# Attention kernel: softmax denominators from probabilities added on VectorE and GpSimd instead of TensorE, and x in one buffer

## The chip, the cores and the metric

The program runs on one core of a Trainium2 chip. The metric is the device time of one execution in microseconds (us); lower is better. PE is TensorE, DVE VectorE, ACT ScalarE, POOL GpSimd, and SP the queue that issues most transfers.

## What is computed

The program is a decoder of six stages: linear plus softmax attention, a graph and router stage, a mixture of experts, a second self-attention, a causal cross-attention with keys and values from a context, and a gated network. The change lies in the second self-attention (four batches of 512 positions, 16 heads of 32) and in the cross-attention (the same sizes, causal). What they compute:

```python
# self-attention of x after layernorm (four batches)
scores = jnp.einsum('bhqd,bhkd->bhqk', q, k) * scale
p = jax.nn.softmax(scores, axis=-1)
o = jnp.einsum('bhqk,bhkd->bhqd', p, v)
return jnp.einsum('bsd,ed->bse', o, w_o)
...
# cross-attention, keys and values from the context
scores = jnp.einsum('bhqd,bhkd->bhqk', qh, kh) * inv_sqrt_d
scores = jnp.where(causal, scores, jnp.finfo(scores.dtype).min)
attn = jax.nn.softmax(scores, axis=-1)
out = jnp.einsum('bhqk,bhkd->bhqd', attn, vh)
```

## The kernel before, in words

Both stages are one function, `attention_layers`. It runs 32 **steps** g: batch b = g // 4 (0 to 3 self-attention, which I call plain; 4 to 7 cross-attention, causal) and c = g % 4, a group of four heads. Each step has eight **half-tiles** s: key tile t = s // 2 and pair of heads w = s % 2. All engines run written-out orders over g and s; semaphores tie them together.

In half-tile s of step g, PE issues `scores_kq(g, s)` (keys on partitions, L440), then `scores_qk(g + 1, s)` for the next step (queries on partitions, L420, in causal steps with a mask product, L425), and then `half(g, s - 2)`: for even s it is `weigh`, four products of the probabilities of one key tile with v (L454); for odd s it is `add_up`, four products of the same probabilities with ones (L463), which sum them over the keys. The last two halves of a step fall into half-tiles 0 and 1 of the next. Behind half-tile 7, `turn_maxima` (L431) turns the row maxima of step g + 1, and `project(g + 3)` makes queries and keys of step g + 3 (L50 to L52).

DVE takes the row maxima of every qk pair (`maxima`, L657). When the last is out, PE may turn them: `turn_maxima` waits for `maxima(g + 1, 7)`. Between the maxima DVE has the reciprocals of the sums of step g - 1 (L682, half-tiles 2 to 5), in steps with c = 0 the layernorm statistics of the next batch (L635, half-tiles 2 to 5), and in steps with c = 1 the residual additions, the normalisation (L649) and the low halves of the turned x (L718). ACT takes the exponentials of every kq pair into `probs` (L572), which has two buffers of a key tile. POOL multiplies the weighed values by the reciprocals (`at_oT`, L766), and in causal steps clears what lies above the diagonal (L750).

The scores, projections, values and outputs share three pairs of PSUM banks in turn. A kq pair is free when ACT has taken its exponential, a qk pair when DVE has its maxima, and PE can run no further ahead than that: the qk pair of half-tile s reuses the banks of the kq pair of s - 1, and the kq pair of s those of the qk pair of s - 2. PE has extra work in some half-tiles (`UNITS`): outputs of the previous batch (L532) in steps with c = 1, the turn of x (L496) there too, and v of the next batch in half-tile 3 of the steps with c = 2 and c = 3.

The x of a batch lies in one of two buffers of 1 MB, `shared_x`.

## Time and profile before

| what | value |
|---|---|
| median of 3 runs | 2982.72 us (2970.9 to 2985.78) |
| profiled execution | 2978.98 us, of which the span of the trace is 2977.2 us |
| the two stages in the trace | about 1500 to 2435 us of the span |
| PE busy in them, from 1600 to 2300 us | 93 to 98 us of each 100 |
| DVE busy there | 52 to 62 us of each 100 |

Times in rows are microseconds from the start of the span. In a row of the timeline the first number is the start, the second the duration, then engine, line, operation and tiles; a bracket at its end gives how long the engine sat idle before it and what released it. A record of the form `x8` on L454 or L463 is one group of four products (each is recorded as two passes). Instructions of one engine overlap a little at their ends, so a start-to-start distance is the better price of one in a row of many.

### The profile page before, as it was taken

What the parts mean: (1) busy time and instruction counts of PE and PEld (TensorE: products, weight loads), DVE (VectorE), ACT (ScalarE), POOL (GpSimd) and SP (SyncE); (2) the same over time, 40 slices, a digit from 0 to 9 for tenths busy, and PEclk for the clock granted to TensorE, in tenths of its full rate; (3) what the DMA queues carried; (4) which work ended last, traced back from release to release, by engine and by line L of the source; (5) the groups of instructions that cost most, each with busy time, mean ns of one, the idle gap of its engine ahead of it and who ended that gap; (6) DMA issues with size and microseconds to landing.
All of it is one profiled execution on the core that took longest, in us unless ns stands there. A gap on an engine that the chain in (4) does not pass through costs nothing. (4 is left out here: it accounts for less than half of the span.)

```text
span 2977.2 us, 34561 instructions
## 1 busy us (share of the span) xinstructions
PE 2487.6 (84%) x12822; PEld 1650.5 (55%) x12822; DVE 1776.5 (60%) x2764; ACT 1224.9 (41%) x1859; POOL 833.9 (28%) x1064
## 2 busy tenths in 40 slices
PE   5898989874443458888859999999999879999999
PEld 4454545422222248778744554545655448888887
DVE  3766666636799956777736555555565444444443
ACT  3443444326767624444404333433433223333332
POOL 2222223214567637888700000001221110000000
PEclk8999999985666679999979999999999989999999
DMA  3313132203232348999842322334433432101000
GB/s 112 73 44 85 44 86 47 71 25 98 79 106 79 126 167 219 261 250 254 193 107 72 86 79 68 100 82 107 115 98 90 120 111 81 43 1 43 1 29 15
DMA packets 177289, 287.62 MB, mean 97 GB/s; under 512 B 20785, under 2 KB 52401, under 8 KB 177138
## 3 DMA queue, kind: packets, MB, share of 16 engines
q1 hardware_dynamic: 159730, 250.25, 28.4%
q0 software_dynamic: 14336, 34.61, 5.8%
q8 instruction: 88, 1.44, 0.2%
q10 hardware_dynamic: 3072, 0.79, 0.1%
q14 instruction: 63, 0.52, 0.1%
HBM read 149.79 MB, written 59.51 MB: 70 GB/s over the span
## 5 line engine op out<-in xcount | busy, mean ns | idle before, releaser
L657 DVE TENSOR_REDUCE at_negmax<-at_ps 128x2 f32<-128x1024 f32 (+3 forms) x256 | 259.2, 1017 | 131.2 <-PE at_ps L420 66.6
L572 ACT ACTIVATE at_probs<-at_ps 128x1024 f32<-128x1024 f32 (+3 forms) x256 | 221.8, 866 | 264.7 <-PE at_ps L440 262.1
L1258 DVE TENSOR_REDUCE a_negmax<-a_ps 128x2 f32<-128x1024 f32 x128 | 155.1, 1217 | 135.8 <-PE a_ps L1011 135.2
L50 PE MATMUL ff_ps<-ff_xnT_hi,ff_s_hi 128*128 128x512 f32 x512 | 201.0, 393 | 5.1 <-DVE ff_xnT_lo L2750 5.1
L52 PE MATMUL ff_ps<-ff_xnT_hi,ff_s_lo 128*128 128x512 f32 x512 | 200.2, 391 | 0.0
L51 PE MATMUL ff_ps<-ff_xnT_lo,ff_s_hi 128*128 128x512 f32 x512 | 200.1, 391 | 0.0
L1841 ACT ACTIVATE gr_act_signs<-gr_signed,gr_test 128x512 bf16<-128x512 f32 x248 | 177.3, 717 | 25.0 <-POOL gr_test L2204 13.4
L1159 ACT ACTIVATE a_probs<-a_ps 128x1024 f32<-128x1024 f32 x128 | 130.9, 1024 | 136.0 <-PE a_ps L1029 135.5
L2780 DVE TENSOR_TENSOR ff_hid<-ff_hid,ff_ps 128x512 f32<-128x512 f32 x64 | 44.0, 688 | 238.7 <-ACT ff_hid L2725 238.7
L440 PE MATMUL at_ps<-at_qk 98*128 98x512 f32 (+3 forms) x512 | 171.7, 417 | 17.4 <-DMA at_qk<-at_mrow 10.9
L50 PE MATMUL ex_ps<-ex_x_hi,ex_gu_hi 128*128 128x256 f32 x512 | 150.8, 294 | 35.7 <-issue 35.7
L440 PEld LDWEIGHTS at_ps<-at_qk 98*128 98x128 f32 x512 | 82.9, 193 | 158.8 <-issue 89.8
L420 PE MATMUL at_ps<-at_qk 96*128 96x512 f32 (+3 forms) x512 | 160.7, 377 | 11.6 <-DVE at_xnT_lo L718 8.0
L2725 ACT ACTIVATE ff_hid<-ff_ps 128x512 f32<-128x512 f32 x64 | 38.3, 598 | 303.5 <-PE ff_ps L52 303.5
L766 POOL TENSOR_TENSOR at_oT<-at_weighed 128x512 f32<-128x512 f32 x32 | 40.8, 1274 | 385.2 <-DVE at_weighed L682 385.2
L51 PE MATMUL ex_ps<-ex_x_lo,ex_gu_hi 128*128 128x256 f32 x512 | 148.1, 289 | 0.0
L52 PE MATMUL ex_ps<-ex_x_hi,ex_gu_lo 128*128 128x256 f32 x512 | 147.9, 289 | 0.0
L750 POOL TENSOR_SCALAR_AFFINE_SELECT at_probs<-at_probs 128x256 f32<-128x256 f32 x128 | 52.6, 412 | 290.9 <-ACT at_probs L572 290.9
L2505 POOL DMA_INDIRECT ex_rows<-normed,index x64 | 117.4, 1835 | 48.4 <-DVE ex_gates L2451 22.6
L682 DVE RECIPROCAL at_weighed<-at_weighed 128x128 f32<-128x128 f32 x128 | 119.9, 940 | 15.1 <-ACT at_weighed L607 15.1
L727 DVE TENSOR_TENSOR at_part<-at_ps,at_part 128x512 fp32r<-128x512 f32 x64 | 43.4, 692 | 142.7 <-ACT at_part L628 142.7
L2440 DVE TENSOR_TENSOR ex_gu_lo<-first_gu,ex_gu_hi 128x2048 fp32r<-128x2048 f32 x32 | 101.0, 3156 | 42.5 <-ACT ex_gu_hi L2404 42.5
(411 smaller groups left out, 6503.3 us busy)
## 6 DMA issues: line engine op xcount, KB each, us to landing
at_qk<-at_part SPq DMA_DIRECT2D x384, 128.0 KB, 2.3
first_gu<-in_L_ffn_w_gate_up_dram SPq DMA_DIRECT2D x32, 1024.0 KB, 5.9
a_qk<-a_part SPq DMA_DIRECT2D x192, 128.0 KB, 2.3
first_d<-in_L_ffn_w_down_dram SPq DMA_DIRECT2D x32, 512.0 KB, 7.0
gr_aside_raw<-in_L_ffn_W_dram SPq DMA_DIRECT2D x48, 256.0 KB, 3.3
w13T<-gr_aside_out SPq DMA_DIRECT2D x32, 256.0 KB, 3.3
shared_x<-x_after_cross SPq DMA_DIRECT2D x8, 1024.0 KB, 8.0
ff_slab<-w13T SPq DMA_DIRECT2D x14, 512.0 KB, 6.9
```

Source lines behind the costliest of these rows:

```text
L50: pe.matmul(out, lh, rh, start=start, stop=False, skip_group_check=True)
L51: pe.matmul(out, lh, rl, start=False, stop=False, skip_group_check=True)
L52: return pe.matmul(out, ll, rh, start=False, stop=stop, skip_group_check=True)
L420: mm = pe.matmul(bank(key, i, 0, n), qk[0:KROWS, g % STACKS, 0, j, t * P:(t + 1) * P], qk[0:KROWS, g % STACKS, 1, j, 0:n], start=True, sto ...
L440: mm = pe.matmul(bank(key, i, lo), qk[0:KROWS + 2, g % STACKS, 1, j, t * P:(t + 1) * P], qk[0:KROWS + 2, g % STACKS, 0, j, lo:S], start=Tr ...
L572: act.activation(probs[:, t % 2, 2 * w:2 * w + 2, lo:S], banks(("kq", g, s), lo), ACT.Exp, scale=SCALE).then_inc(free(("kq", g, s)), 1)
L657: dve.reduce_max(negmax[:, g % 2, :].rearrange("p (j t) -> p j t", t=NT)[:, 2 * w:2 * w + 2, t], banks(("qk", g, s), 0, width(g, t)), AX.X ...
L682: dve.reciprocal(weighed[:, 1, t * P:(t + 1) * P], weighed[:, 1, t * P:(t + 1) * P]).then_inc(rec_done, 1)
L1159: act.activation(probs[:, t % 2, 2 * w:2 * w + 2, :], banks(("kq", g, s)), ACT.Exp, scale=SCALE).then_inc(free(("kq", g, s)), 1)
L1258: dve.reduce_max(negmax[:, g % 2, :].rearrange("p (j t) -> p j t", t=NT)[:, 2 * w:2 * w + 2, t], banks(("qk", g, s)), AX.X, negate=True).t ...
L1841: act.activation(act_signs[:, j, :], src, ACT.Sign, scale=-1.0, bias=against, accum_out=total[:, i, j:j + 1]).then_inc(counted_to[j], 1)
L2505: pool.indirect_dma_start(rows[:, u, t, :], None, normed, slots_of(index, e, t)).then_inc(rows_in[u].sem, 16)
```

## The change

The probabilities of a step's four key tiles are added elementwise into a new tile `total`, the heads of w = 0 by POOL (L797 of the changed kernel), those of w = 1 by DVE (L708), in three additions each (t = 1, 2, 3; the first adds tiles 0 and 1). PE then makes a single product with ones, over `total`, where the last `add_up` stood, in half-tile 1 of the next step (L476). Causal steps keep one small product for the first 128 queries (L466), which see key tile 0 alone; `total` holds the other 384 columns. `total` takes the place of the second x buffer, so x has one buffer, and its loads move: the load of batch b + 2 is issued in step c = 2 of batch b instead of batch b + 3 in step c = 3. The last residual goes into `total`. Exponentials now also wait until the addition that reads their buffer is done.

```diff
-        XS = 2
-        xs_in, ctx_loaded = [sem(f"xs_in{i}") for i in range(XS)], sem("ctx_loaded")
+        xs, xs_in, ctx_loaded = xs_all[:, 0], sem("xs_in"), sem("ctx_loaded")
...
-        probs = sb("probs", [P, 2, QUAD, S])
+        probs, total = sb("probs", [P, 2, QUAD, S]), xs_all[:, 1]
...
+        def total_operands(g, t, w):
+            heads, cols = slice(2 * w, 2 * w + 2), slice(first(g, t), S)
+            return total[:, heads, cols], (probs[:, 0, heads, cols] if t == 1 else total[:, heads, cols]), probs[:, t % 2, heads, cols]
...
             load(sp, 0)
-            load(sp, 1)
...
                     load_residual(b, 0)
                     if b == ALL - 1:
-                        load_residual(b, 1)
                         load_for_network()
+                if g == G:
+                    load_last_residual()
...
-                if c == 3 and 2 <= b + 3 < ALL:
+                if c == 2 and 1 <= b + 2 < ALL:
                     sp.wait_ge(xT_ready, 2 * (b + 2))
...
+            def add_up(g):
+                lo = P if causal(g) else 0
+                if g >= 1:
+                    pe.wait_ge(sums_out, g)
+                pe.wait_ge(pool_totalled, (NT - 1) * (g + 1))
+                pe.wait_ge(dve_totalled, (NT - 1) * (g + 1))
+                for j in range(QUAD):
+                    mm = pe.matmul(ps[j * HD:(j + 1) * HD, SUMS, lo:S], ones[:], total[:, j, lo:S], start=True, stop=True, skip_group_check=True)
                 mm.then_inc(sums_done, 1)
 
             def half(g, n):
                 if n % 2 == 0:
                     weigh(g, n // 2)
-                else:
-                    add_up(g, n // 2)
+                elif n == 1 and causal(g):
+                    sum_first_keys(g)
+                elif n == PAIRS - 1:
+                    add_up(g)
...
                 if NT * g + t >= 2:
-                    act.wait_ge(sums_done, NT * g + t - 1)
+                    act.wait_ge(values_done, NT * g + t - 1)
+                    h, u = (g, t - 2) if t >= 2 else (g - 1, t + 2)
+                    act.wait_ge((pool_totalled, dve_totalled)[w], (NT - 1) * h + max(u, 1))
...
+            def add_to_total(g, t):
+                wait_drained(dve, "kq", g, 2 * t + 1)
+                if causal(g):
+                    dve.wait_ge(masked, PAIRS * (g - NC * B) + 2 * t + 2)
+                if t == 1:
+                    if g:
+                        dve.wait_ge(sums_done, sums_before(g))
+                else:
+                    dve.wait_ge(dve_totalled, (NT - 1) * g + t - 1)
+                out, a, b = total_operands(g, t, 1)
+                dve.tensor_tensor(out, a, b, ALU.add).then_inc(dve_totalled, 1)
...
                     if has(g + 1):
                         maxima(g + 1, s)
+                    if has(g) and s in (4, 6):
+                        add_to_total(g, s // 2 - 1)
...
                 if has(g + 1):
                     maxima_rows(g + 1)
+                if has(g):
+                    add_to_total(g, NT - 1)
...
-                for s in range(PAIRS if has(g) and causal(g) else 0):
-                    mask_diagonal(g, s)
...
+                for s in range(PAIRS):
+                    if has(g) and causal(g):
+                        mask_diagonal(g, s)
+                    if has(g) and s in (2, 4, 6):
+                        add_to_total(g, s // 2)
```

Three places show how the order moves. The first is DVE in step g = 8 (c = 0, plain), from the maxima of half-tile 3 to those of half-tile 7. Before:

```order
L657 TENSOR_REDUCE at_negmax<-at_ps 128x2
L682 RECIPROCAL at_weighed<-at_weighed 128x128
L635 BN_STATS at_stats<-shared_x 128x6
L657 TENSOR_REDUCE at_negmax<-at_ps 128x2
L682 RECIPROCAL at_weighed<-at_weighed 128x128
L635 BN_STATS at_stats<-shared_x 128x6
L657 TENSOR_REDUCE at_negmax<-at_ps 128x2
L682 RECIPROCAL at_weighed<-at_weighed 128x128
L635 BN_STATS at_stats<-shared_x 128x6
L657 TENSOR_REDUCE at_negmax<-at_ps 128x2 x2
L664 CAST at_mrow<-at_ps 16x128
```

And after, from the maxima of half-tile 4 (L675 is `maxima`, L708 the addition, L712 the reciprocal, L653 the statistics, L682 the first of the maxima rows):

```order
L675 TENSOR_REDUCE at_negmax<-at_ps 128x2
L708 TENSOR_TENSOR shared_x<-at_probs 128x1024
L712 RECIPROCAL at_weighed<-at_weighed 128x128
L653 BN_STATS at_stats<-shared_x 128x6
L675 TENSOR_REDUCE at_negmax<-at_ps 128x2
L712 RECIPROCAL at_weighed<-at_weighed 128x128
L653 BN_STATS at_stats<-shared_x 128x6
L675 TENSOR_REDUCE at_negmax<-at_ps 128x2
L708 TENSOR_TENSOR shared_x<-shared_x,at_probs 128x1024
L675 TENSOR_REDUCE at_negmax<-at_ps 128x2
L682 CAST at_mrow<-at_ps 16x128
L684 TENSOR_TENSOR at_mrow<-at_ps,at_mrow 16x128
```

Two of the three additions of DVE now stand ahead of the last maxima, for which PE waits; the third comes behind the rows of the maxima.

The second place is PE in the same step, from half-tile 3 on. Before:

```order
L440 MATMUL at_ps<-at_qk 128x512 x2
L420 MATMUL at_ps<-at_qk 128x512 x2
L463 MATMUL at_ps<-at_probs,at_ones 32x512 x4
L440 MATMUL at_ps<-at_qk 128x512 x2
L420 MATMUL at_ps<-at_qk 128x512 x2
L454 MATMUL at_ps<-at_probs,at_v 32x512 x4
```

And after (L444 and L424 are the two kinds of scores, L458 is `weigh`):

```order
L444 MATMUL at_ps<-at_qk 128x512 x2
L424 MATMUL at_ps<-at_qk 128x512 x2
L444 MATMUL at_ps<-at_qk 128x512 x2
L424 MATMUL at_ps<-at_qk 128x512 x2
L458 MATMUL at_ps<-at_probs,at_v 32x512 x4
```

The products with ones have gone from half-tiles 3, 5 and 7; the one of half-tile 1 stays, with `total` as its operand.

The third place is POOL in two plain steps. Before, there was one multiplication a step:

```order
L766 TENSOR_TENSOR at_oT<-at_weighed 128x512 x3
L744 TENSOR_TENSOR at_rstd<-at_mv,minus_half 128x4
L766 TENSOR_TENSOR at_oT<-at_weighed 128x512 x3
L750 AFFINE_SELECT at_probs<-at_probs 128x2x128 x8
L766 TENSOR_TENSOR at_oT<-at_weighed 128x512
```

And after:

```order
L797 TENSOR_TENSOR shared_x<-at_probs 128x1024
L797 TENSOR_TENSOR shared_x<-shared_x,at_probs 128x1024 x2
L815 TENSOR_TENSOR at_oT<-at_weighed 128x512
L797 TENSOR_TENSOR shared_x<-at_probs 128x1024
L797 TENSOR_TENSOR shared_x<-shared_x,at_probs 128x1024 x2
```

The multiplication of step g - 1 now stands behind the three additions of step g.

## Rows read from the trace of the kernel before

**Rows 1.** The page: length of the span.

```profile
span 2977.2 us, 34561 instructions
```

**Rows 2.** Busy time of each engine in 100 us of plain steps, granted clock (PEclk).

```profile
core 0: us, PE busy (x) PEld busy (x) DVE busy (x) ACT busy (x) POOL busy (x), PEclk, DMA share, GB/s
1700.00:1800.00 100.00, 97.75 (x468) 51.67 (x460) 51.97 (x57) 35.42 (x41) 3.83 (x3) 0.98 0.30 81
```

**Rows 3.** Timeline of PE, step c = 3, from half-tile 4 on.

```profile
1781.19 0.63 PE L440 MATMUL at_ps<-at_qk 98*128 98x512 f32 x2
...
1784.36 1.07 PE L463 MATMUL at_ps<-at_probs,at_ones 128*32 128x512 f32 x8
1785.35 0.74 PE L440 MATMUL at_ps<-at_qk 98*128 98x512 f32 x2
...
1790.03 0.28 PE L431 MATMUL at_ps<-ident,at_negmax 128*16 128x128 f32 x1 [0.32 <-DVE at_negmax L657]
```

**Rows 4.** Timeline of DVE, the same half-tiles.

```profile
1782.33 1.23 DVE L657 TENSOR_REDUCE at_negmax<-at_ps 128x2 f32<-128x1024 f32 x1 [5.65 <-PE at_ps L420]
...
1788.74 1.23 DVE L657 TENSOR_REDUCE at_negmax<-at_ps 128x2 f32<-128x1024 f32 x1 [0.91 <-PE at_ps L420]
```

**Rows 5.** Timeline of ACT: the exponential of half-tile 4 there.

```profile
1782.30 1.03 ACT L572 ACTIVATE at_probs<-at_ps 128x1024 f32<-128x1024 f32 x1
```

**Rows 6.** Timeline of DVE, step c = 0, half-tiles 2 to 7.

```profile
1801.16 1.23 DVE L657 TENSOR_REDUCE at_negmax<-at_ps 128x2 f32<-128x1024 f32 x1 [0.88 <-PE at_ps L420]
...
1803.16 0.64 DVE L635 BATCH_NORM_STATS2 at_stats<-shared_x 128x6 f32<-128x512 f32 x1
...
1811.30 2.33 DVE L657 TENSOR_REDUCE at_negmax<-at_ps 128x2 f32<-128x1024 f32 x2
```

**Rows 7.** Timeline of PE at the end of that step.

```profile
1813.69 0.28 PE L431 MATMUL at_ps<-ident,at_negmax 128*16 128x128 f32 x1 [0.89 <-DVE at_negmax L657]
```

**Rows 8.** Groups of instructions: additions of 128x1024, inputs in SBUF, on POOL and DVE.

```profile
L1397 POOL TENSOR_TENSOR a_raw<-a_raw,a_cosT 128x1024 f32<-128x1024 f32 x8 | 19.1, 2388 | 0.0
...
L2477 DVE TENSOR_TENSOR shared_x<-shared_x 128x1024 f32<-128x1024 f32 x24 | 29.1, 1212 | 1.3 <-DMA w_mixed<-shared_x 1.3
```

**Rows 9.** Timeline of the experts: one DVE subtraction alone, and beside one of POOL.

```profile
1158.48 2.28 DVE L2440 TENSOR_TENSOR ex_gu_lo<-first_gu,ex_gu_hi 128x2048 fp32r<-128x2048 f32 x1
...
1167.38 4.45 DVE L2440 TENSOR_TENSOR ex_gu_lo<-first_gu,ex_gu_hi 128x2048 fp32r<-128x2048 f32 x1 [1.32 <-ACT ex_gu_hi L2404]
...
1166.70 2.97 POOL L2490 TENSOR_TENSOR ex_d_lo<-first_d,ex_d_hi 128x1024 fp32r<-128x1024 f32 x1
```

**Rows 10.** Timeline of PE, causal step: one group with ones, 384 columns.

```profile
2098.86 0.85 PE L463 MATMUL at_ps<-at_probs,at_ones 128*32 128x384 f32 x8
2099.64 0.44 PE L440 MATMUL at_ps<-at_qk 98*128 98x128 f32 x2
```

**Rows 11.** Timeline of DVE, causal step c = 0, half-tiles 2 to 7.

```profile
2133.10 0.69 DVE L657 TENSOR_REDUCE at_negmax<-at_ps 128x2 f32<-128x512 f32 x1 [0.97 <-PE at_ps L425]
...
2141.64 2.33 DVE L657 TENSOR_REDUCE at_negmax<-at_ps 128x2 f32<-128x1024 f32 x2
```

**Rows 12.** Timeline of PE around one fall of the granted clock, step c = 1.

```profile
1851.60 0.73 PE L420 MATMUL at_ps<-at_qk 96*128 96x512 f32 x2 [1.02 <-DVE at_xnT_lo L718]
...
1853.97 0.77 PE L50 MATMUL at_ps<-at_xnT_hi,at_wq_hi 128*128 128x512 f32 x1
...
1855.38 0.63 PE L50 MATMUL at_ps<-at_xnT_hi,at_wq_hi 128*128 128x512 f32 x1
1855.81 0.63 PE L51 MATMUL at_ps<-at_xnT_lo,at_wq_hi 128*128 128x512 f32 x1
...
1857.38 0.39 PE L52 MATMUL at_ps<-at_xnT_hi,at_wq_lo 128*128 128x512 f32 x1
1857.61 0.40 PE L50 MATMUL at_ps<-at_xnT_hi,at_wq_hi 128*128 128x512 f32 x1
```

**Rows 13.** Windows, the same stretch.

```profile
1840.00:1860.00 20.00, 18.44 (x83) 10.63 (x82) 9.04 (x10) 5.49 (x6) 1.71 (x3) 0.91 0.13 41
```

More of the change, by code:

```diff
@@ L346, in load_residual, with load_last_residual @@
                 sp.dma_start(res[:], mid_pairs[b - B, u] if cross(b) else in_pairs[b, u]).then_inc(res_in, 16)
+            def load_last_residual():
+                sp.wait_ge(sums_done, sums_before(G))
+                sp.dma_start(total[:, 0:2, :], mid_pairs[B - 1, 1]).then_inc(last_in, 16)
             def store(b, u):
@@ L388, in _ @@
                     store(b - 1, 0)
-                    if b < ALL:
+                    if (b - 1, 1) != LAST:
                         load_residual(b - 1, 1)
                     store(b - 1, 1)
-                if c == 3 and 2 <= b + 3 < ALL:
+                if c == 2 and 1 <= b + 2 < ALL:
                     sp.wait_ge(xT_ready, 2 * (b + 2))
-                    if cross(b + 3):
-                        sp.wait_ge(res_out, 16 * 2 * (b + 3 - B + 1))
-                    load(sp, b + 3)
+                    if cross(b + 2):
+                        sp.wait_ge(res_out, 16 * 2 * (b + 2 - B + 1))
+                    load(sp, b + 2)
                 if g == NC * (B - 2) + 1:
@@ L456, in weigh, with sum_first_keys @@
                 mm.then_inc(values_done, 1)
-            def add_up(g, t):
-                lo = first(g, t)
-                if t == 0 and g >= 1:
+            def sum_first_keys(g):
+                if g >= 1:
                     pe.wait_ge(sums_out, g)
                 for j in range(QUAD):
-                    mm = pe.matmul(ps[j * HD:(j + 1) * HD, SUMS, lo:S], ones[:], probs[:, t % 2, j, lo:S],
-                                   start=t == 0, stop=t == NT - 1, skip_group_check=True)
+                    mm = pe.matmul(ps[j * HD:(j + 1) * HD, SUMS, 0:P], ones[:], probs[:, 0, j, 0:P], start=True, stop=True, skip_group_check=True)
+                mm.then_inc(sums_done, 1)
+            def add_up(g):
+                lo = P if causal(g) else 0
+                if g >= 1:
+                    pe.wait_ge(sums_out, g)
[3 more added lines that the diff above has]
+                    mm = pe.matmul(ps[j * HD:(j + 1) * HD, SUMS, lo:S], ones[:], total[:, j, lo:S], start=True, stop=True, skip_group_check=True)
                 mm.then_inc(sums_done, 1)
@@ L570, in exponentials @@
                 if NT * g + t >= 2:
-                    act.wait_ge(sums_done, NT * g + t - 1)
+                    act.wait_ge(values_done, NT * g + t - 1)
+                    h, u = (g, t - 2) if t >= 2 else (g - 1, t + 2)
+                    act.wait_ge((pool_totalled, dve_totalled)[w], (NT - 1) * h + max(u, 1))
+                    if u == 0 and causal(h):
+                        act.wait_ge(sums_done, sums_before(h) + 1)
                 act.activation(probs[:, t % 2, 2 * w:2 * w + 2, lo:S], banks(("kq", g, s), lo), ACT.Exp, scale=SCALE
@@ L706, in _ @@
                             dve.wait_ge(last_in, 16)
-                            kept = xs(b)[:, 0:2, :]
+                            kept = total[:, 0:2, :]
                         else:
@@ L751, in mask_diagonal, with add_to_total @@
                                    pattern=[[0, 2], [1, P]], channel_multiplier=-1).then_inc(masked, 1)
+            def add_to_total(g, t):
+                wait_drained(pool, "kq", g, 2 * t)
+                if causal(g):
+                    pool.wait_ge(masked, PAIRS * (g - NC * B) + 2 * t + 1)
+                if t == 1:
+                    if g:
+                        pool.wait_ge(sums_done, sums_before(g))
+                else:
+                    pool.wait_ge(pool_totalled, (NT - 1) * g + t - 1)
+                out, a, b = total_operands(g, t, 0)
+                pool.tensor_tensor(out, a, b, ALU.add).then_inc(pool_totalled, 1)
             rstds(0)
@@ L759, in _ @@
                                        pattern=[[-1, P]], channel_multiplier=1).then_inc(masks_made, 1)
-                for s in range(PAIRS if has(g) and causal(g) else 0):
-                    mask_diagonal(g, s)
-                if has(g - 1):
-                    pool.wait_ge(rec_done, NT * g)
-                    if g - 1 >= NC:
-                        pool.wait_ge(y_ready, 2 * ((g - 1) // NC))
-                    pool.tensor_tensor(oT[:, (g - 1) % NC, :], weighed[:, 0, :], weighed[:, 1, :], ALU.mult).then_inc(o_done, 1)
+                for s in range(PAIRS):
[3 more added lines that the diff above has]
+                        add_to_total(g, s // 2)
+                    if has(g - 1) and s == PAIRS - 1:
+                        pool.wait_ge(rec_done, NT * g)
+                        if g - 1 >= NC:
+                            pool.wait_ge(y_ready, 2 * ((g - 1) // NC))
+                        pool.tensor_tensor(oT[:, (g - 1) % NC, :], weighed[:, 0, :], weighed[:, 1, :], ALU.mult).then_inc(o_done, 1)
                 if g % NC == 0 and 1 <= g // NC + 1 < ALL:
```

27 lines of the change are left out of this document (12 added, 15 removed).

## The prediction

> **What bounds the kernel now.** I read the page for the span [rows 1], then the windows over the two attention stages: in a plain stretch PE is busy 97.75 us of 100, DVE 51.97, POOL 3.83 [rows 2]. By shares alone PE is the bound and the others have room. The shares mislead, because they average over a step. The timelines by engine show the inside of one. In half-tiles 4 to 7 of a step with c = 3, PE runs from 1781.19 to the turn of the maxima at 1790.03, and waits only 0.32 us there for DVE [rows 3]. DVE begins at 1782.33 and has its last maxima from 1788.74, before which it sat idle once, for 0.91 us [rows 4]. So in 8.8 us DVE has about 1 us to spare. In a step with c = 0 it has none: from the maxima of half-tile 2 at 1801.16 its rows follow without a gap until 1811.30 + 2.33 = 1813.63 [rows 6], and PE, done with its last sums, waits 0.89 us for it [rows 7]. DVE's idle time lies elsewhere: while PE makes projections, v and outputs. Work can't be moved there, since the three pairs of banks let PE run ahead by one or two half-tiles only.
>
> **What is removed.** A group of products with ones over 512 columns costs PE 0.99 us (1784.36 to 1785.35) [rows 3], one over 384 columns 0.78 (2098.86 to 2099.64) [rows 10]. By the slope of these two, 256 columns take 0.57 and 128 take 0.36, as an estimate. A plain step goes from four groups to one: 2.97 us less. A causal step has 0.99 + 0.78 + 0.57 + 0.36 = 2.70 and keeps 0.36 + 0.78: 1.56 less. With 16 steps of each, PE loses 47.5 + 25.0 = 72.5 us of work.
>
> **What is added.** Three additions a step on DVE and three on POOL, of 128x1024 in plain steps; 768, 512 and 256 columns in causal ones. The nearest rows with both inputs in SBUF are 1212 ns on DVE and 2388 ns on POOL [rows 8]. On DVE I take 1.14 us start to start, and by width 0.87 and 0.60 for 768 and 512 columns (an estimate: 0.07 of overhead and the columns in proportion). The third addition lies behind the maxima rows, where DVE waits for projections anyway: nothing. If that cover were gone it would cost another 1.14.
>
> *Steps with c = 0, plain (g = 4, 8, 12).* DVE has no gap, so its two additions ahead of the last maxima are 2.3 us on the path, and the three groups removed from PE only make PE wait longer. That is +2.3 before contention.
>
> *Steps with c = 2 and 3, plain (seven without g = 15).* In half-tile 3 one group goes, and PE reaches v 0.99 earlier. Behind v, DVE's work is 1788.74 - 1782.33 - 0.91 = 5.50, then 1.23 for the last maxima [rows 4], and now 2.28 of additions: it ends at 1782.33 + 9.01 = 1791.34 instead of 1789.97. That is +1.4 - 1.0 = +0.4 before contention.
>
> *Contention of DVE and POOL.* A DVE subtraction of 128x2048 with both inputs in SBUF took 2.28 us alone and 4.45 where it started at 1167.38, inside a POOL operation that ended at 1166.70 + 2.97 = 1169.67 [rows 9]. 1169.67 - 1167.38 + 2.2 is 4.5: DVE stood still until POOL was done. The same will meet the additions. In the step with c = 3 POOL's second addition can start when the exponential of half-tile 4 ends, at 1782.30 + 1.03 = 1783.33 [rows 5]; DVE wants its first at 1782.33 + 1.14 = 1783.47. If POOL is first, DVE is late by 2.3 us. If DVE is first, POOL is late, and its third addition meets DVE's second, some 1.8 us. I take 2.0 for c = 2 and 3: together +2.4 a step, with 0.4 and 3.1 as ends. In c = 0 the two meet for less: DVE's first addition is due three maxima, two reciprocals and two statistics after 1801.16, near 1807.4, when POOL's second is nearly over by the same count (0.3), and its second addition meets POOL's multiplication (0.7). I take 1.0: +3.3 a step.
>
> The Trainium skill (SBUF — State Buffer, section Who interferes with whom) says that a DVE instruction with two SBUF inputs and a GpSimd instruction that reads SBUF exclude each other for the whole instruction. By that, the trace agrees in its 4.45 us. Its rule gives the sum that is made here; the page's advice to share such work between the two engines only where one is off the path speaks against this change.
>
> *Steps with c = 1, plain (g = 5, 9, 13).* The outputs leave DVE time; one group of PE is gained, 1.0. The one behind the outputs is lost again to DVE's second addition, ahead of the low halves of x: -1.0 a step. Step 1 has no outputs, so I price it as c = 0: +3.0; step 0 has no reciprocals: +0.5. Step 15 takes the narrow maxima of the first causal step, where PE is the bound: -2.0.
>
> Plain: 3 x 3.3 + 7 x 2.4 - 3 x 1.0 + 3.0 + 0.5 - 2.0 = **+25.2 us**.
>
> *Causal steps.* With c = 0 DVE has no gap from 2133.10 to 2143.97 [rows 11]; two additions are 0.87 + 0.60 = 1.5, the group in half-tile 1 has 384 columns where it had 128 (+0.4, ahead of DVE's stretch), and contention 0.4: +2.3, four times 9.2. With c = 1: +0.4 in half-tile 1, -0.6 in half-tile 3 (0.99 becomes 0.36), and half of the 0.78 behind the outputs: -0.6, four times -2.4. With c = 2 and 3 the additions cost 1.5, of which some 0.4 lie in a gap, less 0.2 net on PE: +0.9 in five, +0.1 in the two that turn a weight, where the gap is longer: 4.7. Step 31 has no maxima to take, and PE keeps its gain: -1.5. Causal: **+10.0 us**.
>
> *The granted clock.* PE now waits for DVE for some 4 us at a stretch ahead of the turn of the maxima in 12 plain steps (all but those with outputs), and about 2 in 11 causal ones. In the trace of before, a step where PE waited 1.02 us and then again ran into a stretch where its products follow at 0.43 us (1855.38, 1855.81) instead of 0.23 (1857.38, 1857.61) [rows 12], the window at 0.91 [rows 13]: at 1.2 GHz instead of 2.4. From 1853.97 to 1857.38 there are eight products, which would take 8 x 0.235 = 1.9 us at full clock and took 3.4: 1.5 us lost. I price one such fall in each of the 12 and one in every second of the 11: 1.5 x 17.5 = **+26.3 us**. The ends are 0 (no further fall) and two falls in each of the 12, 12 x 3 + 11 x 1.5 = 52.
>
> **The sum.** 25.2 + 10.0 + 26.3 = +61.5 us. Against the profiled execution of 2978.98 (its span 2977.2 and 1.8 around it) this is 3040.5; the median of the runs, 2982.72, is 3.7 above that execution, so I forecast 3044, and with the terms this rough **3043 us**.
>
> **What hides the rest.** The loads of x: one buffer is enough, since the load of batch b + 2 waits only for the turn of x in half-tile 6 of the step before, and its statistics come two steps later. If that cover were gone, each of seven loads would show by what it takes to land. Queued behind it on SP are the 12 transfers of a stack, which are needed a whole step later. The wait of ACT for additions: the exponential of half-tile 5 can't start before DVE's first addition ends, and behind it stands that of half-tile 6; PE needs both for the banks of the next qk pairs, and is ahead of DVE by then. POOL has 3 x 2.39 = 7.2 us of additions and one multiplication of half that width in a step whose second half alone takes PE 8.8 us: the multiplication comes late, but it is needed only in half-tile 1 of the step after next.
>
> **Rivals.**
> 1. *DVE is the bound but without contention and without further falls of the clock.* For it: DVE's order might let the additions miss each other. The sum is then 3 x 2.3 + 7 x 0.4 - 3 x 2.0 + 2.3 + 0.2 - 2.0 = +4.2 plain, and causal 10.0 - 1.6 = +8.4: 2995. Against it: 1783.33 and 1783.47 lie 0.14 apart. Chance 0.15.
> 2. *Contention, but the clock holds*: +35.2, 3018. For it: the wait of 0.89 us [rows 7] was not followed by slow products. Chance 0.25.
> 3. *The other side: PE's time counts in full.* If PE ran further ahead than I think, DVE's wait at the end of a step would shrink, and up to 72.5 us would be gained; it decides where DVE's stretch of a step is shorter than PE's. With half of it, 2946. Against it: the unbroken stretch of 12.5 us [rows 6], to which 2.3 are added. Chance 0.07.
> 4. *POOL becomes the bound*, every addition of DVE blocked for a full 2.39 twice a step: 28 x 4.8 is 134 on top of the adds, 3110 to 3130. It decides if POOL is late by more than one addition. Chance 0.08.
>
> The forecast itself (contention and falls of the clock, 3020 to 3075) has 0.45.
>
> **The numbers.** A measurement tells 0.5%, or 15 us, from no change. The range runs from 2992, the first rival, to 3085, part way to the fourth: 0.8. Slower by over 0.5% (above 2998) holds the forecast, the second and fourth rival and a part of the first: 0.83. Within 0.5%: 0.11. Faster: 0.06.
>
> **What would show it.** PE: no L463, one group a step at L476 (and L466), with PE's busy share in plain windows falling from 98 to some 85. DVE: from 52 to some 65 of 100, and no gap ahead of the last maxima in steps with c = 0, 2 and 3. The turn of the maxima (L435) waits for L675 by 3 to 5 us in plain steps, by 2 in causal ones. Additions on DVE (L708) have a mean well above 1.2 us, up to 3.6 in single rows; those on POOL from 2.4. The granted clock in the attention windows is below 0.98. The forecast is wrong if the turn waits less than 1 us, or L708 has a mean of 1.2, or PE's share stays above 93.

## The result: 3.3% slower

The changed kernel takes 3073.9 us (median of 4 runs, 3071.6 to 3076.24); the kernel before took 2978.85 (4 runs, 2970.9 to 2985.78) beside it. The ratio is 1.033, with a 95% interval from 1.031 to 1.035. The forecast was 3043 us, 31 us too low. The page's span and the windows of the changed kernel, in the columns of [rows 1, 2, 13]:

```profile
span 3074.5 us, 33727 instructions
1700.00:1800.00 100.00, 85.94 (x339) 48.21 (x343) 62.96 (x73) 31.32 (x37) 24.35 (x12) 0.86 0.26 70
1840.00:1860.00 20.00, 16.59 (x65) 9.94 (x66) 12.94 (x23) 6.32 (x9) 4.62 (x3) 0.74 0.10 24
```

PE is busy 86 of 100 us where it was 98, and it is slower while it works: the granted clock is 0.86 there, where it was 0.98. The second window shows 0.74 for 0.91, but it isn't the same work: the changed kernel is some 33 us behind by then and still at the end of step 8, while the kernel before was already at the end of step 9. DVE rose from 52 to 63 and POOL from 4 to 24.

To see where the 97.3 us of span went, I cut each step in two by PE's rows. One part is **behind the turn**: from the turn of the maxima (L435) to the next step's first kq product (L444), mostly the projections. The other is the **body**, from there to the next turn. Over the 31 steps that have a next turn, these parts are 28.2 and 67.1 us longer than before; the remaining 2 us lie ahead of and behind them. By kinds of steps, with the forecast's terms for the same steps:

| part | forecast | measured |
|---|---|---|
| behind the turns (granted clock) | +26.3 | +28.2 |
| plain c = 0 (g = 0, 4, 8, 12) | +10.4 | +12.7 |
| plain c = 1 (g = 1, 5, 9, 13) | 0.0 | +7.8 |
| plain c = 2 and 3 | +14.8 | +19.4 |
| causal c = 0 | +9.2 | +10.1 |
| causal c = 1 | -2.4 | +11.9 |
| causal c = 2 and 3 (without g = 31) | +4.7 | +5.2 |

**Behind the turn.** PE at the end of the step whose end before was shown in [rows 7], and at the start of its projections:

```profile
1846.95 0.38 PE L435 MATMUL at_ps<-ident,at_negmax 128*16 128x128 f32 x1 [3.27 <-DVE at_negmax L675]
1847.06 0.77 PE L50 MATMUL at_ps<-at_xnT_hi,at_wq_hi 128*128 128x512 f32 x1
1847.62 0.63 PE L51 MATMUL at_ps<-at_xnT_lo,at_wq_hi 128*128 128x512 f32 x1
...
1851.89 0.58 PE L52 MATMUL at_ps<-at_xnT_hi,at_wq_lo 128*128 128x512 f32 x1
1852.30 0.39 PE L50 MATMUL at_ps<-at_xnT_hi,at_wk_hi 128*128 128x512 f32 x1
1852.54 0.40 PE L51 MATMUL at_ps<-at_xnT_lo,at_wk_hi 128*128 128x512 f32 x1
```

The wait of 0.89 us is now 3.27, and the twelve products behind it follow at 0.43 us, the pace of 1.2 GHz in [rows 12]; the others, from 1852.30, at 0.23. The granted clock in these two stretches:

```profile
1847.00:1852.30 5.30, 5.30 (x13) 4.16 (x14) 1.69 (x3) 0.00 (x0) 0.00 (x0) 0.50 0.02 6
1852.30:1857.00 4.70, 4.70 (x25) 2.99 (x23) 1.74 (x8) 2.10 (x3) 0.00 (x0) 1.00 0.00 0
```

**The body of a plain step with c = 2** (g = 10): DVE, POOL, ACT and PE around half-tiles 4 and 5.

```profile
1904.99 1.23 DVE L675 TENSOR_REDUCE at_negmax<-at_ps 128x2 f32<-128x1024 f32 x1
1906.13 0.94 DVE L712 RECIPROCAL at_weighed<-at_weighed 128x128 f32<-128x128 f32 x1
1911.54 1.23 DVE L675 TENSOR_REDUCE at_negmax<-at_ps 128x2 f32<-128x1024 f32 x1 [4.46 <-PE at_ps L424]
1912.68 3.40 DVE L708 TENSOR_TENSOR shared_x<-at_probs 128x1024 f32<-128x1024 f32 x1
```
```profile
1912.63 2.37 POOL L797 TENSOR_TENSOR shared_x<-shared_x,at_probs 128x1024 f32<-128x1024 f32 x1 [6.72 <-ACT at_probs L590]
```
```profile
1916.19 1.94 ACT L590 ACTIVATE at_probs<-at_ps 128x1024 f32<-128x1024 f32 x2 [3.64 <-DVE shared_x L708]
```
```profile
1917.27 1.22 PE L424 MATMUL at_ps<-at_qk 96*128 96x512 f32 x2 [3.17 <-ACT at_probs L590]
```

The rows to look at are the third and the fourth: DVE stood idle for 4.46 us, took the maxima of half-tile 4, and only then began its first addition, 0.05 us behind one of POOL's. It took 3.40 us. The exponential of half-tile 5 waited for it, since it overwrites what is being added, and the next qk product waited for that exponential's bank. In the whole trace this wait of L424 on ACT is 43.5 us; the forecast had priced it at nothing.

**The body of a causal step with c = 1** (g = 21): DVE, POOL, PE.

```profile
2232.39 3.93 DVE L667 TENSOR_SCALAR shared_x<-shared_x,at_mv,at_rstd 128x512 f32<-128x512 f32 x4
2236.24 0.68 DVE L675 TENSOR_REDUCE at_negmax<-at_ps 128x2 f32<-128x512 f32 x1
```
```profile
2231.57 1.83 POOL L797 TENSOR_TENSOR shared_x<-at_probs 128x768 f32<-128x768 f32 x1
...
2234.78 1.26 POOL L797 TENSOR_TENSOR shared_x<-shared_x,at_probs 128x512 f32<-128x512 f32 x1
```
```profile
2237.07 8.80 PE L546 MATMUL at_ps<-at_wo,at_oT 128*128 128x512 f32 x16 [2.12 <-DVE at_negmax L675]
```

In the kernel before, the same two places in this step are, on DVE and on PE:

```profile
2160.69 1.90 DVE L649 TENSOR_SCALAR shared_x<-shared_x,at_mv,at_rstd 128x512 f32<-128x512 f32 x4
```
```profile
2163.45 7.13 PE L532 MATMUL at_ps<-at_wo,at_oT 128*128 128x512 f32 x16
```

The four normalisations took 3.93 us beside POOL's additions, where they had taken 1.90. The maxima behind them were late, PE waited 2.12 us for them ahead of the outputs, and then ran 16 products in 8.80 us in place of 7.13. Together that is the +3.8 us of this step; g = 17 and 25 are longer by 3.9 and 3.8. Step 29 has outputs and additions too, but no next batch to normalise, and its body is only 0.4 us longer.

### The profile page after: what moved, and what is told of

It reads as the page before. It is cut to its first block and busy times, and to the rows that moved or that the text cites. A ratio compares the mean times of both kernels' runs of the same rounds, so it can differ in the third digit from the quotient of the medians.

```text
span 3074.5 us, 33727 instructions
## 1 busy us (share of the span) xinstructions
PE 2477.5 (81%) x12182; PEld 1672.3 (54%) x12182; DVE 1897.6 (62%) x2860; ACT 1223.1 (40%) x1859; POOL 1028.7 (33%) x1160
## 5 line engine op out<-in xcount | busy, mean ns | idle before, releaser
L675 DVE TENSOR_REDUCE at_negmax<-at_ps 128x2 f32<-128x1024 f32 (+3 forms) x256 | 257.1, 1007 | 109.7 <-PE at_ps L424 54.9
L424 PE MATMUL at_ps<-at_qk 96*128 96x512 f32 (+3 forms) x512 | 170.8, 398 | 56.4 <-ACT at_probs L590 43.5
L444 PE MATMUL at_ps<-at_qk 98*128 98x512 f32 (+3 forms) x512 | 173.8, 423 | 27.9 <-DMA at_qk<-at_mrow 10.1
L444 PEld LDWEIGHTS at_ps<-at_qk 98*128 98x128 f32 x512 | 86.2, 199 | 152.9 <-issue 72.1
L797 POOL TENSOR_TENSOR shared_x<-shared_x,at_probs 128x1024 f32<-128x1024 f32 (+1 forms) x64 | 112.8, 1763 | 130.1 <-ACT at_probs L590 125.3
L797 POOL TENSOR_TENSOR shared_x<-at_probs 128x1024 f32<-128x1024 f32 (+1 forms) x32 | 67.5, 2108 | 250.3 <-ACT at_probs L590 248.1
L424 PEld LDWEIGHTS at_ps<-at_qk 96*128 96x128 f32 x512 | 100.6, 201 | 85.1 <-ACT at_probs L590 53.6
L546 PE MATMUL at_ps<-at_wo,at_oT 128*128 128x512 f32 x256 | 121.3, 630 | 16.5 <-DVE at_negmax L675 10.8
```

The costliest lines, as they stand in the source:

```text
L424: mm = pe.matmul(bank(key, i, 0, n), qk[0:KROWS, g % STACKS, 0, j, t * P:(t + 1) * P], qk[0:KROWS, g % STACKS, 1, j, 0:n], start=True, sto ...
L444: mm = pe.matmul(bank(key, i, lo), qk[0:KROWS + 2, g % STACKS, 1, j, t * P:(t + 1) * P], qk[0:KROWS + 2, g % STACKS, 0, j, lo:S], start=Tr ...
L546: mm = pe.matmul(bank(key, i), oT[:, dc, t * P:(t + 1) * P], woT[:, dc, :], start=dc == 0, stop=dc == NC - 1, skip_group_check=True)
L675: dve.reduce_max(negmax[:, g % 2, :].rearrange("p (j t) -> p j t", t=NT)[:, 2 * w:2 * w + 2, t], banks(("qk", g, s), 0, width(g, t)), AX.X ...
L797: pool.tensor_tensor(out, a, b, ALU.add).then_inc(pool_totalled, 1)
```

## The experiments

All of these ran beside the kernel before, whose medians were 2975.64 to 2977.58 us; given are medians, ratios with 95% intervals, and the parts' difference from the kernel before in us, by the cut above. Base for comparison: the changed kernel has 28.2 behind the turns and 12.7, 7.8, 19.4, 10.1, 11.9 and 5.2 in the bodies.

| run | us | ratio | behind turns | plain c=0 | c=1 | c=2, 3 | causal c=0 | c=1 | c=2, 3 |
|---|---|---|---|---|---|---|---|---|---|
| no_adds | 2971.65 | 0.9988 [0.9978, 0.9998] | 20.7 | -1.4 | -2.1 | -16.1 | -0.1 | 0.0 | -5.8 |
| pool_narrow | 3031.11 | 1.0193 [1.0174, 1.0212] | 35.5 | 7.4 | 2.7 | -2.6 | 7.3 | 0.6 | 4.0 |
| dve_narrow | 3032.27 | 1.0191 [1.0172, 1.0210] | 32.4 | 4.3 | 4.1 | 3.7 | 4.2 | 8.1 | -0.4 |
| x_single | 2975.16 | 0.9992 [0.9978, 1.0007] | -0.3 | 1.4 | 0.1 | 0.1 | 0.1 | 0.0 | 0.5 |
| pool_narrow_c1 | 3061.12 | 1.0281 [1.0260, 1.0301] | 28.2 | 12.6 | 2.3 | 18.7 | 11.2 | 0.6 | 5.1 |
| warm | 3049.77 | 1.0237 [1.0218, 1.0255] | -3.0 | 19.9 | 8.1 | 22.3 | 15.8 | 6.9 | 5.3 |
| no_adds_warm | 2953.60 | 0.9913 [0.9894, 0.9931] | 1.9 | 0.1 | -2.0 | -16.1 | -0.1 | -0.1 | -5.9 |
| early | 3059.02 | 1.0264 [1.0245, 1.0284] | 41.0 | 15.9 | 7.5 | -5.2 | 7.0 | 6.9 | 2.4 |
| early_warm | 3025.80 | 1.0157 [1.0136, 1.0178] | 15.8 | 14.5 | 9.9 | -5.2 | 6.8 | 10.2 | -2.1 |
| pairs23 | 2968.24 | 0.9971 [0.9955, 0.9988] | -0.8 | 0.0 | 0.0 | -9.8 | 0.1 | 0.0 | 0.6 |
| triple23 | 2959.59 | 0.9938 [0.9920, 0.9956] | -2.7 | 0.1 | 0.0 | -15.9 | 0.1 | 0.0 | 0.4 |
| triple_all | 2961.01 | 0.9942 [0.9920, 0.9963] | -1.0 | 1.6 | 0.0 | -16.0 | 0.1 | 0.0 | -2.1 |

### no_adds: what is PE's time worth?

```diff
-                for j in range(QUAD):
-                    mm = pe.matmul(..., ones[:], total[:, j, lo:S], ...)
+                for j in range(QUAD):
+                    mm = pe.matmul(..., ones[:], probs[:, 1, j, lo:S], ...)
...
-                        add_to_total(g, s // 2 - 1)
```

> The changed kernel without any addition: VectorE and Pool do none of them, nothing waits for them, and PE's one product with ones reads the probabilities of key tile 1 as they stand. Most of the sums is left out; everything else, the single buffer of x too, is as in the changed kernel. Theory A (the additions cost the time, by their length on Pool and by keeping VectorE from its own work, and the shorter product with ones gives back little because PE waits at the turn of maxima for VectorE): about 2941 us, 2925 to 2955, that is about 133 us under the changed kernel and only 38 under the one before. Rival B (each microsecond that PE is spared is a microsecond won): 72 us under the one before, 2907. Rival C (it is not the additions but the moved loads of x and the granted clock that falls since PE has less to do): still above 2979.

It took 2971.65 us: 4 under the kernel before, not 38 and not 72. None of the three theories had the number: A's 2925 to 2955 was too low, and C's, above 2979, too high, though the clock that C names is there. The bodies became 25.6 us shorter: 21.9 of it in steps with c = 2 and 3, 2.1 in plain ones with c = 1, and none with c = 0 but for g = 0, whose body differs by as much between runs that share its instructions (1.3 us more in `x_single`). Behind the turns 20.7 us were lost again. PE's row there, as before and without additions, in the view of groups:

```profile
L431 PE MATMUL at_ps<-ident,at_negmax 128*16 128x128 f32 x32 | 9.3, 290 | 24.6 <-DVE at_negmax L657 24.6
```
```profile
L435 PE MATMUL at_ps<-ident,at_negmax 128*16 128x128 f32 x32 | 9.8, 305 | 53.4 <-DVE at_negmax L674 53.4
```

The wait at the turn grew from 24.6 to 53.4 us. So PE's shorter work was hardly worth anything even with the additions for free: it became waiting, and the waiting cost clock (`no_adds_warm` below).

### pool_narrow and dve_narrow: whose additions?

```diff
-                out, a, b = total_operands(g, t, 0)
+                out, a, b = (ap[:, :, 0:16] for ap in total_operands(g, t, 0))
```

(in `dve_narrow` the same for VectorE's, `total_operands(g, t, 1)`)

> The changed kernel with Pool's additions cut to 16 columns of each head; all instructions and waits stay, VectorE's additions are whole. The sums of two heads of four are left incomplete. Theory A (Pool's long additions exclude VectorE's additions and its normalisation of x, so that the maxima come late): VectorE's additions fall to about 1.2 us each, the four normalisations of a causal step with c=1 from 3.9 us to under 2.5 us, and the time is 2955 to 2985, about 105 us under the changed kernel. Rival D (VectorE's own additional work is what makes it late, with or without Pool): at most 30 us under the changed kernel, 3045 or more.

> The changed kernel with VectorE's additions cut to 16 columns of each head; Pool's additions are whole. The sums of the two other heads are left incomplete. Theory A: Pool still excludes the normalisation and the reciprocals' neighbours, and its additions of 2 us each stand in its queue, but nothing of 1.2 to 3.4 us stands ahead of the maxima: 2990 to 3025, about 65 us under the changed kernel. Rival D (VectorE's own additional work is the cause): about 2950, as without any addition. Rival E (Pool's own queue is the bound): within 20 us of the changed kernel, 3055 or more.

Neither theory had the sizes: 3031 and 3032, each some 42 us under the changed kernel and 60 over `no_adds`, where theory A had up to 2985 and up to 3025. Against `no_adds` the bodies are 45.0 us longer with DVE's additions alone, 49.6 with POOL's alone and 92.7 with both, so that the two nearly add up. They weigh differently by steps: DVE's own work most in the steps with c = 0 (14.7 us over the kernel before, against 8.5 with POOL's alone); POOL's in the steps with c = 1, 8.1 us in the causal ones, where DVE's alone leave 0.6. How POOL's cost arises is plain in the groups of DVE, first of `after`, then of `pool_narrow`, then of `dve_narrow`:

```profile
L708 DVE TENSOR_TENSOR shared_x<-at_probs 128x1024 f32<-128x1024 f32 x16 | 36.1, 2259 | 0.0
L667 DVE TENSOR_SCALAR shared_x<-shared_x,at_mv,at_rstd 128x512 f32<-128x512 f32 x36 | 25.7, 775 | 2.3 <-POOL at_rstd L778 2.3
```
```profile
L708 DVE TENSOR_TENSOR shared_x<-at_probs 128x1024 f32<-128x1024 f32 x16 | 19.9, 1242 | 0.0
L667 DVE TENSOR_SCALAR shared_x<-shared_x,at_mv,at_rstd 128x512 f32<-128x512 f32 x36 | 16.8, 531 | 2.3 <-POOL at_rstd L778 2.3
```
```profile
L708 DVE TENSOR_TENSOR shared_x<-at_probs 128x32 f32<-128x32 f32 x32 | 28.4, 887 | 2.7 <-ACT at_probs L590 2.7
L667 DVE TENSOR_SCALAR shared_x<-shared_x,at_mv,at_rstd 128x512 f32<-128x512 f32 x36 | 25.7, 774 | 2.3 <-POOL at_rstd L778 2.3
```

With POOL's additions short, DVE's of 128x1024 take 1242 ns in place of 2259, and the normalisations 531 in place of 775. With DVE's short and POOL's whole, a DVE addition of 128x32 takes 887 ns in the mean. One of them, and POOL beside it:

```profile
1890.11 2.36 DVE L708 TENSOR_TENSOR shared_x<-at_probs 128x32 f32<-128x32 f32 x1
```
```profile
1890.06 2.37 POOL L797 TENSOR_TENSOR shared_x<-shared_x,at_probs 128x1024 f32<-128x1024 f32 x1 [6.73 <-ACT at_probs L590]
```

It ended 0.04 us behind POOL's: DVE stood still, small as its own work was. `dve_narrow` therefore doesn't take DVE's waiting away, which is why it was slower than I expected. The Trainium skill (SBUF — State Buffer, section Who interferes with whom) lists `tensor_scalar`, under conditions on its operands, beside the operations with two SBUF inputs among those that can exclude GpSimd and be excluded. The normalisation is a `tensor_scalar`, and the 531 and 775 ns agree.

### x_single: the loads

```diff
-        XS = 2
-        xs_in, ctx_loaded = [sem(f"xs_in{i}") for i in range(XS)], sem("ctx_loaded")
+        xs, xs_in, ctx_loaded = xs_all[:, 0], sem("xs_in"), sem("ctx_loaded")
...
-                if c == 3 and 2 <= b + 3 < ALL:
+                if c == 2 and 1 <= b + 2 < ALL:
```

> The kernel before with x in a single buffer and its loads moved as in the change, and nothing else; the sums are those of the kernel before. Theory A (the loads land long before the statistics need them): within 5 us of the kernel before, 2974 to 2984. Rival C (the loads come late in the steps with c=0 of the changed kernel and hold up the statistics and the normalisation): 10 us or more above it.

2975.16 against 2975.64: the single buffer costs nothing that can be measured.

### pool_narrow_c1: the normalisation

```diff
-                out, a, b = total_operands(g, t, 0)
+                out, a, b = (ap[:, :, 0:16] if g % NC == 1 else ap for ap in total_operands(g, t, 0))
```

> The changed kernel with Pool's additions cut to 16 columns of each head in the steps with c = 1 alone, the steps in which VectorE normalises x; Pool's additions are whole in the 24 other steps. The sums of two heads of four are left incomplete in eight steps. Theory A (the steps with c = 1, mis-sized in the forecast, are long because Pool's additions exclude the normalisation and the additions on VectorE): the bodies of these steps fall from 19.7 us over the kernel before to about 3.3, as with all of Pool's additions cut, and the time by 12 to 20 us against the changed kernel, to 3054 to 3062. Rival (something else of the steps with c = 1, VectorE's own additional work or the later loads of x): less than 6 us, above 3068.

The bodies with c = 1 fell from 19.7 us to 2.9, the others stayed, and the time fell by 12.8 us, as its theory A had it. All 36 normalisations are at full speed again:

```profile
L667 DVE TENSOR_SCALAR shared_x<-shared_x,at_mv,at_rstd 128x512 f32<-128x512 f32 x36 | 16.8, 531 | 2.3 <-POOL at_rstd L778 2.3
```

### warm and no_adds_warm: the granted clock

```diff
+                if has(g) and has(g + 1):
+                    filler(g, 3 if g % NC == 0 else 1)
                 if has(g + 1):
                     turn_maxima(g + 1)
```

`filler(g, n)` makes n times four products with ones, over a constant. In `no_adds_warm` n is 1.

> The changed kernel with more work on PE that nobody needs: just before the turn of the maxima it makes one product with ones over a constant for each head (three in the steps with c = 0), into the bank of the sums, which is free then. Nothing of the reference is left out. Theory F (the granted clock falls in the projections and outputs because PE has just waited at the turn of the maxima for VectorE): the part of a step from the turn to the first kq product, 28 us over the kernel before in sum, falls to under 12 us over it, the bodies gain under 10 us from the additional products, and the time is 3055 to 3070. Rival (the clock falls by what PE does in a much longer stretch, or the waits are too short to matter): this part stays at 22 us or more over the kernel before, and the time rises by the length of the products that lie beside no wait, 3080 or more.

> The kernel without any addition (most of the sums left out), with one product with ones over a constant for each head just before the turn of the maxima in every step. There the part from the turn to the first kq product is 21 us over the kernel before, and the bodies 26 us under it. Theory F: this part falls to under 8 us over it, the bodies rise by up to 12 us where PE had no wait, and the time is 2955 to 2970. Rival: this part stays at 15 us or more over the kernel before and the bodies rise all the same, 2975 or more.

With more work on PE, `warm` is 24 us faster than the changed kernel, and `no_adds_warm` 18 us faster than `no_adds`; both are a little below the range that theory F gave. The part behind the turns is 3.0 us under the kernel before instead of 28.2 over it, and 1.9 instead of 20.7. The turn of g = 8 in `warm`, with the filler ahead of it (L485):

```profile
1842.93 3.42 PE L485 MATMUL at_ps<-ident,at_ones 128*32 128x512 f32 x24
1846.28 0.28 PE L435 MATMUL at_ps<-ident,at_negmax 128*16 128x128 f32 x1
1846.31 0.47 PE L50 MATMUL at_ps<-at_xnT_hi,at_wq_hi 128*128 128x512 f32 x1
...
1848.96 0.40 PE L52 MATMUL at_ps<-at_xnT_hi,at_wq_lo 128*128 128x512 f32 x1
1849.20 0.39 PE L50 MATMUL at_ps<-at_xnT_hi,at_wk_hi 128*128 128x512 f32 x1
```

The twelve products take 1849.20 - 1846.31 = 2.89 us; in the changed kernel they took 1852.30 - 1847.06 = 5.24. The granted clock from 1846.30 to 1849.20 is 1.00 in `warm`, where the changed kernel had 0.50. The bodies grew by 11.2 us against the changed kernel, above all with c = 0, where three fillers were longer than the wait that they filled. The outputs give the same answer: in g = 17, PE waits 2.12 us ahead of the second eight tiles' products in both kernels,

```profile
2131.13 8.80 PE L546 MATMUL at_ps<-at_wo,at_oT 128*128 128x512 f32 x16 [2.12 <-DVE at_negmax L675]
```
```profile
2121.89 7.11 PE L555 MATMUL at_ps<-at_wo,at_oT 128*128 128x512 f32 x16 [2.12 <-DVE at_negmax L686]
```

and they take 8.80 us in the changed kernel (above) and 7.11 in `warm` (below), although the filler lies not here but at the ends of the steps. The granted clock in the first 3 us of them is 0.70 (2131 to 2134) and 1.00 (2121.9 to 2125). That the clock's fall costs this much is shown; what exactly lets it fall in one place and not in the next isn't.

### early and early_warm: the place of the first addition

```diff
-                    if has(g) and s in (4, 6):
-                        add_to_total(g, s // 2 - 1)
+                    if has(g) and s == 6:
+                        add_to_total(g, 2)
...
+                    if has(g) and s == 3:
+                        add_to_total(g, 1)
```

> The changed kernel with VectorE's first addition of a step moved up by one place in its queue, from behind the maxima of half-tile 4 to behind those of half-tile 3. The trace of the changed kernel shows VectorE idle for 4.46 us ahead of the maxima of half-tile 4 in a plain step with c = 2, with the exponentials of half-tile 3 done; then the addition takes 3.40 us beside one of Pool, an exponential waits for it and a qk product 3.17 us for the exponential. Nothing of the reference is left out. Theory A (in plain steps with c = 2 and 3 the chain addition, exponential, qk product, maxima is the bound): seven bodies of c = 2 and 3, 19.4 us over the kernel before, fall to under 8 us over it, and the time by 12 to 25 us against the changed kernel, 3049 to 3062. Rival (the addition only waits for the exponentials at its new place and holds up the maxima of half-tile 4 in turn, or these bodies are long by the work on VectorE as such): less than 6 us either way, 3068 to 3080.

> Both at once: the addition moved up as in the run named early, and one product with ones over a constant for each head just before the turn of maxima in every step, so that PE doesn't stand idle there. Nothing of the reference is left out. If both remedies work on different parts (the bodies of c = 2 and 3; the granted clock behind the turn), their gains add up: 28 us and what the other gives, 3020 to 3040. This is still above the kernel before, since the additions' length in the bodies of c = 0 and c = 1 stays. Rival (it is one cause, and the second remedy finds nothing left): as the better of the two alone, 3045 or more.

`early` is 15 us faster than the changed kernel. The bodies of plain steps with c = 2 and 3 went from 19.4 us over the kernel before to 5.2 under it. DVE in g = 10 again:

```profile
1900.56 1.23 DVE L675 TENSOR_REDUCE at_negmax<-at_ps 128x2 f32<-128x1024 f32 x1
1901.70 0.94 DVE L712 RECIPROCAL at_weighed<-at_weighed 128x128 f32<-128x128 f32 x1
1902.56 1.16 DVE L708 TENSOR_TENSOR shared_x<-at_probs 128x1024 f32<-128x1024 f32 x1
1907.11 1.23 DVE L675 TENSOR_REDUCE at_negmax<-at_ps 128x2 f32<-128x1024 f32 x1 [3.39 <-PE at_ps L424]
```

The addition takes 1.16 us inside DVE's idle time, and PE's wait for ACT at L424 there is 0.18 us in place of 3.17 (2.1 in the whole trace, in place of 43.5). The steps with c = 0, where DVE has no idle time, didn't gain in sum (15.9 and 7.0, before 12.7 and 10.1), and the part behind the turns is longer than ever, by 41.0 us. With the filler as well 3025.8 us are reached: together they gain 48 us, a little more than the 15 and 24 of each alone, and still leave 1.6%.

### pairs23, triple23 and triple_all: additions where PE is the bound

`x_single`, and POOL alone adds key tiles, for all four heads, in plain steps with c = 2 and 3:

```diff
+        def paired(g):
+            return has(g) and not causal(g) and g % NC in (2, 3)
...
+            def add_pair(g, w):
+                wait_drained(pool, "kq", g, 2 + w)
+                if g and w == 0:
+                    pool.wait_ge(sums_done, NT * g)
+                heads = slice(2 * w, 2 * w + 2)
+                pool.tensor_tensor(total[:, heads, :], probs[:, 0, heads, :], probs[:, 1, heads, :], ALU.add).then_inc(pool_totalled, 1)
```

`triple23` has a second function of this kind, which adds key tile 2; `triple_all` does it in causal steps too, with `paired` without its second condition.

> The kernel before with the single buffer of x, and in the eight plain steps with c = 2 or 3 the first two key tiles added up by Pool alone (two additions of 128x1024), so that PE makes three groups of products with ones there in place of four. The additions lie in steps without a normalisation, and VectorE does none. Nothing of the reference is left out. Theory A: these bodies are bound by PE; without any addition three groups less gave 2.0 us in each, so one group less gives about 0.7, and a fall of the granted clock takes up to 1.5 back in some: 2968 to 2978. Rival G (one group less is enough for all of the 2.0 us, since the turn waits for VectorE from there on): 2959 to 2965. Rival H (Pool's additions delay its other work or VectorE's even here): above 2980.

> As the run named pairs23 (the kernel before with a single buffer of x, Pool alone adding in the eight plain steps with c = 2 and 3), with key tile 2 added by Pool too, so that PE makes two groups of products with ones there in place of four. Nothing of the reference is left out. There one group less gave 1.25 us in each of eight bodies and no fall of the granted clock; without any addition three groups less gave 2.0 us. Theory A (PE is the bound of these bodies until the turn waits for VectorE): another 0.3 to 0.7 us in each, less what the clock takes back where PE now waits at the turn, 2960 to 2970, at most 5 us better than pairs23. Rival (Pool's third and fourth addition end so late that an exponential of half-tiles 4 to 7 or of the next step waits for them, or lie beside the turn's small operations on VectorE): above pairs23, 2970 to 2985.

> As the run named triple23, and the same in the eight causal steps with c = 2 and 3: Pool adds key tiles 0, 1 and 2 for all heads there too, between its masks, and PE makes a product of 128 columns, one of 384 and the last key tile's in place of four. Nothing of the reference is left out. Without any addition the bodies of these steps were 5.8 us shorter in sum, and the clock took 4.0 us of it back behind the turn. Theory A (Pool has room in every step with c = 2 and 3): up to 5 us better than triple23 if the clock holds, nothing if it falls, 2954 to 2962. Rival (Pool's additions, between 8 masks in a step of 16 us, delay masks for which the products with v wait, or an exponential): above triple23, 2965 or more.

All three beat both kernels. `pairs23` gave 1.25 us in each of eight bodies, and `triple23` 2.0, which is all that `no_adds` gave there, without a fall of the clock: 2959.59 us, 0.6% under the kernel before; `pairs23` is 0.3% under it, and its interval ends at 0.9988, so that gain is small but there. I had expected less of the third key tile, at most 5 us; the difference between the two runs is 8.7 us, that of their bodies 6. Its windows, beside [rows 2]:

```profile
1700.00:1800.00 100.00, 97.29 (x471) 52.35 (x470) 58.37 (x65) 38.89 (x44) 22.70 (x11) 1.00 0.33 88
```

POOL works 22.7 of 100 us, as in the changed kernel, but PE is still at 97 and its clock at 1.00. Nothing of the additions' cost shows. In these steps DVE has no operation with two SBUF inputs and no normalisation for POOL to exclude, and all its normalisations elsewhere keep their 531 ns:

```profile
L662 DVE TENSOR_SCALAR shared_x<-shared_x,at_mv,at_rstd 128x512 f32<-128x512 f32 x36 | 16.8, 531 | 2.3 <-POOL at_rstd L757 2.3
```

`triple_all` gained 2 us in the causal bodies and lost as much elsewhere: no difference from `triple23`.

## Why it came out as forecast, and where the sum was off

The forecast's mechanism, DVE as the bound with additions ahead of the last maxima, exclusion between DVE and POOL, and a clock that falls behind a waiting PE, is what the runs show. Its sum was +61.5 us; +95 came, within the stated range but a third of it uncounted.

- **The granted clock**: +26.3 forecast, +28.2 measured. I counted 17.5 falls of 1.5 us; 16 parts behind a turn are longer by 1.3 to 2.6. `warm` shows that these are the clock's. That the size fits is partly luck: I expected falls behind waits of some 4 us in plain steps and 2 in causal ones, and they came behind waits of 1.3 to 3.9 us, though not behind each of 1.3. Not counted was that the outputs would fall too (8.80 for 7.13 us).
- **Steps with c = 0**: +19.6 with g = 0, measured +22.8. Step 0 alone is 3.0 of the difference (3.5 for 0.5); the seven others were forecast at 19.1 and are 19.3. Nothing of PE's saving survives here: `no_adds` gives -1.5 over eight steps, all of it in g = 0.
- **Steps with c = 1: the step that failed.** "The outputs leave DVE time; one group of PE is gained": -2.4 over all eight, measured +19.7. Step 1 alone, without outputs, was put at +3.0 and measured +4.6. I had read [rows 9] as a rule for DVE's additions alone and left the normalisation in these very steps out. `pool_narrow_c1` gives 16.8 of the 19.7 back. POOL's additions exclude the normalisation (531 becomes 775 ns in the mean, 3.93 us for four in g = 21). In causal steps PE waits 2.12 us for the maxima behind it and starts its outputs at the lower clock; in plain ones it waits 1.5 us, and the 16 outputs behind it take 7.11 us (g = 9).
- **Steps with c = 2 and 3**: +14.8 plain, measured +19.4, near in size but partly by another chain: that it is near is luck. I wrote that work can't be moved into DVE's idle time while PE makes v. `early` moved it there, and against `no_adds` the additions' cost in these bodies fell from 35.5 us to 10.9. The cost was in the order, first addition behind maxima 4, and in the exponential that waits for it, and it takes POOL to make it this large: with POOL's additions short (`pool_narrow`) and the order unchanged, these bodies are 2.6 us under the kernel before. I had written that PE "is ahead of DVE by then" and priced that wait at nothing.
- **PE's saving**: valued at 1.0 us where I thought it counted. By the bodies of `no_adds` it counts for 2.0 us in each plain step with c = 2 and 3, 0.6 in the plain ones with outputs, some 0.8 in the causal ones with c = 2 and 3, and nothing elsewhere. The third rival, PE's time in full, is refuted by `no_adds`: 4 us instead of the 72.5 that I had estimated.
- **The loads**: free, as forecast. The fourth rival (POOL as the bound) did not come; its additions wait for ACT most of the time.
- By what was to be seen: PE's share 86 (forecast 85), DVE's 63 (65), additions on DVE up to 3.4 us; the turn waits 3.3 us in c = 0, as said, but only 1.3 in g = 10, since the wait had moved ahead to L424.

## What to carry to other kernels

Before work is moved off an engine, remove it without a substitute in an experiment: here that alone would have shown 4 us for some 72 us (the forecast's estimate) of spared products. Move it only in the steps where the engine is truly the bound, and onto an engine whose instructions exclude nothing that the critical chain needs, normalisations with `tensor_scalar` among them; `triple23` is the same idea in eight of 32 steps, and wins. And where a wait is hidden by idle time, look whether the order of the queue lets the work reach it.

## What was not expected of the hardware

- A DVE addition of 128x32 took 2.36 us because POOL had begun one of 128x1024 0.05 us earlier. Here the price of the exclusion was POOL's remaining time, not DVE's size.
- PE with more to do made a slower kernel faster by 24 us: four or twelve products that nobody reads, ahead of the turn, keep the twelve projections behind it at 2.4 GHz (2.89 us instead of 5.24).
- With nothing added at all, PE waits 2.45 us at the turn of g = 8 in place of 0.89, and the clock fell in so many steps that 20.7 of 25.6 us were lost.
